# A hand-ordered attention and feed-forward kernel: a new step order, and stack loads of 4 KB pieces in place of 512 B pieces

## What is computed

```python
x = x + attn_a(LN(x))   # one head of 128; Wqkv 512x384, softmax over 256 keys, Wo 128x512
x = x + ffn(LN(x))      # int4 weights, (w_int - zero) * scale, 512x512, plus bias
x = x + attn_b(LN(x))   # 32 heads of 16, rotary q and k, causal softmax over 256 keys, wo 512x512
x = x + ffn(LN(x))      # the same feed-forward layer again
```

## Time and profile before

| | |
|---|---|
| Three runs | 276.99, 274.87 and 278.05 us; median 276.99 us |
| Profiled execution | 276.74 us, span 275.0 us |
| TensorE busy | 253.9 us, 92% of the span |
| VectorE busy | 230.1 us, 84% |
| GpSimd busy | 185.8 us, 68% |
| ScalarE busy | 143.7 us, 52% |
| DMA | 33.94 MB in 52151 packets |
| Granted TensorE clock | 0.999 of full speed |

### The profile page before, as it was taken

How to read it: one execution, slowest core, us unless ns; L and a number is a source line. 1 busy time by engine, 2 the same in 40 slices (tenths; PEclk the granted TensorE clock), 3 DMA queues, 4 the chain that set the end, 5 groups by cost and what they waited for, 6 DMA issues and landing times.

```text
span 275.0 us, 6466 instructions
## 1 busy us (share of the span) xinstructions
PE 253.9 (92%) x2295; PEld 210.0 (76%) x2295; DVE 230.1 (84%) x416; ACT 143.7 (52%) x237; POOL 185.8 (68%) x226
## 2 busy tenths in 40 slices
PE   5698989899997999978999999999999999998994
PEld 2586867696896988866887888798878787685774
DVE  2587968588997999996999889799799989796896
ACT  5347797646247146544533475844455654456330
POOL 3277889999998967595557858545878454437371
PEclk9999999999999999999999999999999999999999
DMA  6999562003463535333432333444344433102104
GB/s 173 299 387 380 214 215 57 0 0 83 122 170 108 146 107 152 109 110 108 137 113 75 101 99 96 119 133 118 104 121 117 134 99 100 58 3 79 39 0 153
DMA packets 52151, 33.94 MB, mean 123 GB/s; under 512 B 5592, under 2 KB 46744, under 8 KB 52120
## 3 DMA queue, kind: packets, MB, share of 16 engines
q1 hardware_dynamic: 52120, 33.54, 40.6%
HBM read 25.00 MB, written 8.39 MB: 121 GB/s over the span
## 4 chain that ended last, share of the span: by engine, by line
PE 41%; POOL 23%; SPq 13%; issue 7%; DMA 6%; DVE 6%; ACT 2%; POOLq 0%; ACTq 0%; DVEq 0%
SPq L522 11%; PE psum L954 7%; PE psum L955 6%; PE psum L956 6%; POOL X L596 6%; POOL wb_lo L601 5%; PE psum L1133 5%; POOL rstd L577 4%; PE psum L1096 4%; PE psum L1118 3%; PE psum L1048 3%; DMA QK<-qk_parts 2%; PE psum L1049 2%; PE psum L978 2%; DMA qk_parts<-parts 2%
## 5 line engine op out<-in xcount | busy, mean ns | idle before, releaser
L623 POOL TENSOR_SCALAR_AFFINE_SELECT E<-E 128x512 f32<-128x512 f32 x64 | 41.7, 676 | 41.2 <-ACT E L766 41.1
L903 DVE TENSOR_REDUCE nmax<-psum 128x4 f32<-128x512 f32 (+1 forms) x64 | 59.2, 943 | 4.5 <-PE psum L1096 4.2
L766 ACT ACTIVATE E<-psum 128x1536 f32<-128x1536 f32 x32 | 46.3, 1447 | 22.9 <-PE psum L1120 17.4
L954 PE MATMUL psum<-XT_lo,wb_hi 128*128 128x256 f32 x128 | 37.9, 296 | 0.0
L630 ACT ACTIVATE parts<-SH 128x512 bf16<-128x512 f32 x32 | 20.0, 627 | 32.4 <-POOL SH L612 21.8
L955 PE MATMUL psum<-XT_hi,wb_lo 128*128 128x256 f32 x128 | 36.2, 282 | 0.0
L956 PE MATMUL psum<-XT_hi,wb_hi 128*128 128x256 f32 x128 | 36.1, 282 | 0.0
L954 PE MATMUL psum<-wb_lo,XT_hi 128*128 128x256 f32 (+1 forms) x96 | 32.4, 337 | 0.6 <-DVE XT_lo L834 0.6
L1096 PE MATMUL psum<-QK 128*128 128x128 bf16 x256 | 28.8, 220 | 2.2 <-DMA QK<-qk_parts 2.2
L955 PE MATMUL psum<-wb_hi,XT_lo 128*128 128x256 f32 (+1 forms) x96 | 30.6, 319 | 0.0
L956 PE MATMUL psum<-wb_hi,XT_hi 128*128 128x256 f32 (+1 forms) x96 | 30.6, 319 | 0.0
(11 more groups left out here) (119 smaller groups left out, 674.2 us busy)
## 6 DMA issues: line engine op xcount, KB each, us to landing
QK<-qk_parts SPq DMA_DIRECT2D x192, 64.0 KB
qk_parts<-parts SPq DMA_DIRECT2D x16, 384.0 KB, 2.8
X<-L_attn_a_x SPq DMA_DIRECT2D x8, 256.0 KB, 7.9
out<-X SPq DMA_DIRECT2D x6, 256.0 KB, 2.2
wb_raw<-L_attn_b_wq SPq DMA_DIRECT2D x1, 1024.0 KB, 10.0
wb_raw<-L_attn_b_wk SPq DMA_DIRECT2D x1, 1024.0 KB, 12.8
wb_raw<-L_attn_b_wv SPq DMA_DIRECT2D x1, 1024.0 KB, 14.7
QK<-mask_rows SPq DMA_DIRECT2D x8, 128.0 KB
```

The costliest lines, as they stand in the source:

```text
L623: last = nc.gpsimd.affine_select(out=e, in_=e, compare_op=ALU.is_ge, fill=0.0, base=0, pattern=[[0, GH], [1, P]], channel_multiplier=-1)
L766: nc.scalar.activation(E[:, n % 2], bank(3, 3), ACT.Exp, scale=float(HD) ** -0.5).then_inc(done[k], 1)
L903: nc.vector.tensor_reduce(nmax[:, u % 2, g::NG, t], (bank(1, 2) if t else bank(0)).rearrange("p (h k) -> p h k", h=GH), AX, ALU.max, negat ...
L954: nc.tensor.matmul(out_, stat[0], mov[1], start=first, stop=False)
```

## The change

1. The stack loads of a unit are six DMAs instead of twelve. `LOADS` groups the blocks of a stack into three, two and one. For q, one part is read three times, twice or once, by a broadcast of the source; for k, parts 0 to 2, 0 to 1 or 0 are read. The source of each names the copy (or the part) outermost, then the 16 channels, then 2048 values in one run of 4 KB. The bytes loaded are the same.
2. So that the 8 heads of a channel lie in one run of DRAM, the columns of wq and wk are laid out on the host with the channel ahead of the head. The rotary table and the exchange of pairs (`i ^ UH`, which is `i ^ 8`, in place of `i ^ 1`) follow.
3. `PLAN` is in a new order throughout. It has the same steps but one: the five dummy matmuls near the end, `("KP", 5, 0)`, are gone. Of the input loads, `wqkv` 3 now comes first, `wo1` and the weights of attn_b come in another order, and `ww` 3 (wo) stands just ahead of the first store.

```diff
+LOADS = ((0, 3), (3, 2), (5, 1))
 KROWS = HD * len(Q_PARTS)
...
-    pair = (np.arange(P) % HD) // 2
-    sign = np.where(np.arange(P) % 2 == 0, -1.0, 1.0).astype(np.float32)
+    place = np.arange(P) // UH
+    pair = place // 2
+    sign = np.where(place % 2 == 0, -1.0, 1.0).astype(np.float32)
...
 PLAN = [
-    ("D", "xt", 1, 0), ("D", "wqkv", 0), ("D", "xt", 0, 0), ("XH", 1, 0), ("XL", 1, 0), ("QH", 0), ("QL", 0), ("KP", 8),
...
-    ("FS", 4, 3, 0), ("FD", 4, 2, 1), ("FD", 4, 3, 0, 0), ("KP", 5, 0), ("T", 4, 3, 1), ("TH", 4, 3, 1),
...
+    ("D", "wqkv", 3), ("QH", 3), ("QL", 3), ("D", "xt", 1, 0), ("XH", 1, 0), ("D", "wqkv", 0), ("QH", 0), ("KP", 8),
...
+    ("BA", 2, 2, 0), ("SS", 0), ("P1", 2), ("PJ", 3, 1), ("R1", 2), ("RS", 3, 1), ("SL", 0), ("S", 0, 0, 0), ("P2", 2),
...
+    ("VP", 6, 0), ("NB", 9), ("S", 14, 0, 0), ("VP", 6, 1), ("TH", 4, 1, 1), ("TL", 4, 1, 1), ("P3", 15), ("SM", 12),
+    ("EX", 11, 1), ("SS", 15), ("S", 14, 0, 1), ("MK", 11, 0), ("VV", 6), ("MT", 13), ("M1", 13), ("ST", 12, 0),
+    ("PV", 11, 0), ("NX", 10), ("NB", 10), ("M2", 13), ("EX", 12, 0), ("DH", 2, 0, 0), ("MK", 11, 1), ("SM", 13),
+    ("PV", 11, 1), ("MX", 14, 0, 0), ("S", 14, 1, 0), ("MX", 14, 0, 1), ("S", 14, 1, 1), ("ST", 12, 1), ("BA", 4, 1, 0),
...
-            return 16 * (2 + (2 * len(Q_PARTS) + 1) * (u // QK_SLOTS) + 2 * len(Q_PARTS))
+            return 16 * (2 + (2 * len(LOADS) + 1) * (u // QK_SLOTS) + 2 * len(LOADS))
...
-                    for a, (stack, which) in enumerate(((queries(u), Q_PARTS), (keys(u), K_PARTS))):
-                        for row, c in enumerate(which):
-                            sp.dma_start(stack[row * HD:(row + 1) * HD],
-                                         scratch[u % 2, c, a].rearrange("(h d) t -> d h t", d=HD)
-                                         ).then_inc(qk_loaded[u % QK_SLOTS], 16)
+                    for row, n in LOADS:
+                        q, kk = (stack[row * HD:(row + n) * HD].rearrange("p h t -> p (h t)")
+                                 for stack in (queries(u), keys(u)))
+                        part = scratch[u % 2, Q_PARTS[row], 0].rearrange("(d h) t -> d (h t)", d=HD)
+                        sp.dma_start(q, part.unsqueeze(0).to_broadcast((n, HD, UH * S))
+                                     ).then_inc(qk_loaded[u % QK_SLOTS], 16)
+                        sp.dma_start(kk, scratch[u % 2, 0:n, 1].rearrange("c (d h) t -> c d (h t)", d=HD)
+                                     ).then_inc(qk_loaded[u % QK_SLOTS], 16)
...
-                    nc.vector.stream_shuffle(SH[:, u % 2], ps, [i ^ 1 for i in range(32)])
+                    nc.vector.stream_shuffle(SH[:, u % 2], ps, [i ^ UH for i in range(32)])
...
+    for n in ("L0_attn_b_wq", "L0_attn_b_wk"):
+        arrays[n] = np.ascontiguousarray(arrays[n].reshape(C, KT, UH, HD).transpose(0, 1, 3, 2).reshape(C, C))
```

## The result

| | before | changed |
|---|---|---|
| Median of 4 runs | 276.26 us | 378.68 us (376.46 to 382.45) |
| Ratio, 95% interval | | 1.368 [1.355, 1.381] |
| Profiled execution | 276.74 us, span 275.0 us | 377.76 us, span 376.0 us |
| Stores of a unit, issue to landing, min / median / max | 2.7 / 2.8 / 3.7 us | 2.8 / 8.8 / 11.7 us |
| Turns from unit 0's first stack load to unit 15's, mean | 10.5 us | 17.1 us |

The account below looks back on a forecast made before the run. TensorE's own work was taken to bound the kernel before; with confined loads, 81.6 us to unit 0's scores, fifteen turns of 14.9 us, 2 us, a 38.3 us tail and 1.7 us outside, less 1.4 us, gave 346 us, range 275 to 356 us.

Parts of the forecast that it names:

- The three large steps: Stack loads: confined to three or two engines, store queued behind them, 14.9 us per turn setting the units' pace.
- rival B: Units' loop: loads confined, but the store's share does not wait; landing near 3 us, 315 us in all; chance 0.22.
- A: Units' loop, the forecast: loads confined, store waits behind them, landing above 10 us; 346 us, 328 to 355; chance 0.50.
- Rival C: Stack loads dealt evenly over the engines, 2.1 us a unit: faster, 272 us; chance 0.17.
- The sum: Whole span: unit 0's scores at 81.6 us, fifteen turns of 14.9 us, 2 us for SM 13, tail 38.3 us.
- The price of a piece: Stack loads: a 4 KB piece takes 0.172 us (23.8 GB/s), from a straight line through two windows.
- The cheap end of the range: Units' loop: a turn of 13.7 us, from a lone engine at 26.5 GB/s; 328 us in all.
- the dear end: Stack loads: dealt by turns of the outermost loop, so the first engine carries 12.9 us per unit.
- The bounds of -5 and +5 us: New step order: worth -5 to +5 us by itself, and nothing when the loop of stores and loads sets the pace.
- the even deal: Stack loads: 192 pieces of 4 KB over 16 engines take 2.1 us a unit, against 2.7 us before.
- The dummy matmuls: Near the end: they take 1.25 us; removing them gives back 0 to 1.2 us.

Follow-up runs that it names:

- e5: Six merged loads (48, 32 or 16 rows outermost) with the step order of the kernel before: 271.70 us, ratio 0.981 against the kernel before.
- e4: Changed kernel with k's parts stored in reverse, so its six loads have 48, 32 or 16 rows outermost: 269.00 us, 0.969 against the kernel before.
- e1: Changed kernel's six stack loads with the step order of the kernel before: 359.54 us, ratio 1.292 against the kernel before.
- e2: Kernel before, with its twelve loads of 512 B pieces, in the new step order: 290.53 us, ratio 1.050 against the kernel before.
- e3: Changed kernel with each block loaded by itself: twelve loads, 4 KB pieces, 16 rows outermost; 291.76 us, ratio 1.050 against the kernel before.
- e6: Changed kernel with the two-block loads split into single blocks, eight loads, one of three copies per stack: 337.45 us, 1.219 against the kernel before.

## Why the prediction was wrong in size

**Confirmed.** The three large steps came as foretold: the loads of three and two blocks use three and two engines; the store's share waits behind them (rival B refuted: the landing is 8.8 us in the median and 11.7 us for a store issued at once behind its loads, not near 3 us; "above 10 us", the sign named for A, holds for such stores only); one turn on the first engine sets the pace of the units. TensorE's busy share is 75% as named, the DMA's share in the units' stretch fell from 0.41 to 0.24, and the waits for stack loads passed 50 us. Rival C is refuted for these loads. Its 272 us for even dealing is what e5 (271.7) and e4 (269.0) give.

**The sum.** The span was put at 343.9 us and is 376.0 us, 32.1 us more. By the sum's own terms:

| term | forecast | measured | difference |
|---|---|---|---|
| unit 0's scores | at 81.6 us | at 79.9 us | -1.7 |
| twelve regular turns (less 1.4 us of mask rows) | 177.4 us | 189.7 us | +12.3 |
| three long turns (2 us for `SM` 13 foreseen) | 46.7 us | 66.3 us | +19.6 |
| last loads' issue to scores, against the first | the same | 0.2 us more | +0.2 |
| tail behind unit 15's scores | 38.3 us | 40.0 us | +1.7 |

The scores are read from the timeline of TensorE; here those of a unit in the middle, and unit 15's:

```profile
218.89 0.61 PE L1102 MATMUL psum<-QK 128*128 128x128 bf16 x4 [6.36 <-DMA QK<-qk_parts]
...
336.04 0.61 PE L1102 MATMUL psum<-QK 128*128 128x128 bf16 x4 [4.48 <-DMA QK<-qk_parts]
```

**The price of a piece** was mis-sized: 0.172 us by a straight line through two windows, of pieces of 512 B and 2 KB on 16 engines. A regular turn of 15.8 us less the turn's other terms as forecast (0.23 + 1.36 + 1.4 + 0.55 = 3.5 us) leaves 12.3 us for 66 pieces, 0.186 us each; 21 GB/s, the mean of the slices above, gives 0.19 us. The range of the turn ended at 15.5 us, and the turn passed it. The cheap end of the range was a lone engine at 26.5 GB/s, a figure that no row of before gives and that the mean here, 21 GB/s, is far from. No row of before had two or three engines at work alone, so the top should have stood further off. This is 12 of the 32 us.

**The step that failed** is "under the dear end it is worth nothing, because the loop of stores and loads sets the pace and hides it", said of the order. It holds only for turns in which nothing but the loads and the store is waited for. In three turns SP stood at a step that waited for something else, and the DMA share was near zero for 5 to 7 us:

- Into unit 4 SP waited 9.6 us for `ST` 0, which frees the buffer that `SL` 4 fills (L514 below). `ST` 0 in turn waited for the rows of maxima, which were issued from 116.2 us on behind the loads of unit 3 and let `ST` 0 go at 126.5 us; before, such rows landed after 1.9 us in the median.
- Into unit 7 it waited 16.2 us for `P3` 7 (L902), which stood behind the scores of unit 6.
- Into unit 15 it stood at `SM` 13 until 319.7 us, the store having been issued at 309.7 us. The 2 us foreseen were for `MT`, `M1`, `M2` and the issue alone. The scores of unit 14 ahead of them started only at 314.7 us, when its loads had landed, and 3 us of other work of TensorE is listed between.

```profile
SPq L514 <- PE psum L1126: 12.6, 4, 9.6
```

All three are chains from the loads of one unit over computation to the loads of the next, beside the chain over the store that the sum followed. The price of the order under these loads is 18 to 21 us (by the times 359.5 and 377.8 us, or by the ratios 1.292 and 1.368); e1's mean turn, long ones included, is 15.6 us against 17.1 us, and 15 x 1.5 = 22 us. The bounds of -5 and +5 us were put on the order without counting SP's landing waits in each list: the new one puts `SL` next behind its `SS` in 12 of 16 units, and e2, with the whole new order and the loads of before, costs 13 us. That it is this part of the order fits e2's waits and e4's lack of a loss, but no run moved these steps alone. The list of SP steps also passes over unit 7 with "on in this way", where `SM` 5 stands between `SS` 7 and `SL` 7.

**What is late next** was said rightly for SP and not looked at for TensorE. Its matmuls took 283.4 us instead of 253.9 us with five fewer. The granted clock fell from 1.00 to 0.84 in the units' stretch. The chain shows it between the transfers that set the pace: one kind of matmul, first 1.1 us after TensorE had idled for 6.4 us, then 4.9 us after it had begun the scores of the unit at 251.87 us:

```profile
192.48 11.70 DMA qk_parts<-parts
...
207.83 11.01 DMA QK<-qk_parts
...
220.02 0.21 PE psum L962
...
239.94 11.88 DMA QK<-qk_parts
...
256.76 0.12 PE psum L962
```

0.21 and 0.12 us per matmul of 256 columns are the two levels, 1.2 and 2.4 GHz (granted clock 0.50 from 219 to 222 us, 1.00 from 256 to 258 us). In a regular turn this work lies beside the loads. In the long turns it is part of what the late `P3` waits for: in the chain 180 to 184 us is matmuls of 0.21 us each, just ahead of `P3` 7. The stretches of such slow matmuls in the chain of the three long turns are 5.3, 3.3 and 4.1 us long; at the upper level they would take half, so the clock made some 6 us of the 19.6 us, an estimate from these lengths. e4, at a clock of 1.00, still has a gap of 18.7 us into unit 7, which it makes up for with turns of 7.5 to 10.3 us behind it. A loop at its own limit can't make up for anything, and this is the part of the mechanism that my sum had no term for.

**Smaller terms.** Unit 0's first load came 3.4 us earlier than the sum had it (65.4 against 68.8 us), but took 14.5 us to the scores instead of 12.8 us; the second takes back half of the first. Pieces of 4 KB dealt over all 16 engines took 0.32 us each in e4, not 0.172 us, so the even deal's 2.1 us a unit were nearly 4 us; beside TensorE's work that cost nothing, and rival C's 272 us stood all the same. The turns of before, put at 10.9 us, are 10.5 us. The dummy matmuls are worth no more than was said. The exchange by 8 and the host's layout cost nothing that shows: e3, which has both, is within 1.3 us of e2, which has neither.

**Open.** What the late steps around unit 7 cost by themselves, since no run moved them all; what makes e6 slower than its first engine says; and whether the new order is worth anything with e4's loads, since e4 (0.969) is better than e5 (0.981) but its repeat (0.977) is not told apart from it.

## What to carry to other kernels

Look at the outermost dimension of both sides of every transfer: a leading dimension of copies or parts gave the whole transfer to that many DMA engines here, three or two of sixteen, and what follows on them, stores and the small rows too, queued up behind. Merge copies into rows instead (e4 did it by storing one operand's parts in the opposite order), which keeps the saved issues: 269.0 us, 3% faster than before in one pair of medians and 2% in another, and 29% faster than the changed kernel. And a store whose loads come next in the same queue makes landing and issues serial: count that sum per unit against the unit's own time, and with it every other step of the list that stands between one unit's loads and the next; when a serial loop is near its limit, add each late start in full, since later turns can't win it back.

## What the runs showed of the hardware that was not expected

- A DMA engine that works with one or two others moved about 21 GB/s in pieces of 4 KB (57 GB/s on 2.9 engines in one stretch, 21 GB/s for each in the mean of 138 slices).
- The same pieces into 16 to 48 rows on all 16 engines ran at 202 GB/s with a DMA share of 0.98, 13 GB/s for each engine or 0.32 us per piece; input loads ran at 382 GB/s at a share of 1.05. In e4 that is hidden.
- Rows of maxima, 4 KB each, landed after 2.4 us in the median but up to 11.1 us when issued behind confined loads; in the kernel of before the longest took 4.0 us.
- The issue of a load of three copies held SP for 0.7 to 0.8 us, and of a single block 0.4 us; a merged load of e4 took 0.42 us in the median.
